# Five prefix products for fourteen, row statistics stored with the rows, shorter routing and new instruction orders in a four-layer sandwich kernel

## The chip, the cores and the metric

The program runs on one core of one Trainium2 chip. The core has five engines that run at the same time and wait for one another through semaphores: TensorE (PE in the profile, its weight loads PEld), VectorE (DVE), ScalarE (ACT), GpSimd (POOL) and SyncE (SP), which issues most of the DMAs. The metric is the device time of one execution in microseconds, as the median over runs.

## What is computed

The state is x, 8192 rows (tokens) of 256 values in fp32. Four sublayers follow one another; each normalizes x, computes, normalizes the result and adds it to x:

```python
x = x + ln(L0_attn(ln(x)))   # window attention, memory, gate, feed-forward
x = x + ln(L0_ffn(ln(x)))    # 8 experts, at most 512 rows each, GELU
x = x + ln(L1_attn(ln(x)))   # linear attention: relu(q), relu(k), kv = k^T v per batch
x = x + ln(L1_ffn(ln(x)))    # 8 experts, at most 1024 rows each, ReLU
```

Both expert layers route a row to the expert with the largest logit. Its place in the expert's buffer is the number of earlier rows with the same expert, a running count over all rows:

```python
onehot = one_hot(argmax(logits), 8)
rank = sum((cumsum(onehot, axis=0) - onehot) * onehot, axis=-1)
keep = rank < capacity
```

## The kernel before

Rows are handled in 16 groups of 512, a group as four tiles of 128 rows, side by side in one SBUF tile. Matrix products take fp32 operands as a high and a low part (`fh` and `fl`, for instance): ACT copies the high part, DVE subtracts it from the value to get the low part, and PE adds three products (`three`). Every engine has its own program, written out by hand in the order in which its instructions run; nothing reorders them, so a wait of one instruction holds all that stand behind it on that engine. The results of PE go through a ring of three PSUM units (`unit` takes the next one and waits until the third last is free again) and one fixed unit, `acc`.

The stages, one after the other:

- **Memory stage** (to about 270 us): two products and a Gram matrix over all groups.
- **Group loop** (about 270 to 1030 us): steps `s` over 16 groups, in which five groups are worked on at once. Group `s` is in the feed-forward (`ff_in`, `w2`, and DVE's `low`, `added`), group `s+1` at the gate (`gates`, `merged`, `weighed`, `combined`, `stats_2nd`, `affine_2nd`), group `s+2` in the window attention (`scores`, `masked`, `exponent`, `attend`, `attended`, `stats_1st`, `affine_1st`), groups behind `s` at the last norms (`affine_3rd`, `stats_4th`, `new_x`, `stats_5th`) and at the routing: `t_t`, `logits`, `route1` (argmax, one-hot `oht`), `prefix` (counts), `route2` (slots), `scatter` (four indirect DMAs into `d_p`). `doubled` writes the normalized row `df`, which SP stores in `d_x1` (`d_x` in the profile).
- **First expert stage** (about 1040 to 1240 us): eight blocks of 512 rows. `expert_out`, `expert_stats`, `expert_norm` and `expert_sum` make the new rows `eq`, and POOL's `expert_put` scatters them into `d_x1`.
- **Pair loop** (about 1250 to 1625 us): the linear attention, two groups a step. `load_x1` reads rows of `d_x1` as `xA`; `stats_l` and `nmean_l` (DVE) and `root` (POOL) make their mean and scale; `xl_norm` (ACT), `xl_t`, `queries`, `keys`, `state` (the sum kv in `acc`) follow. A pair is a batch: when its kv is complete, `kw_high` (ACT) and `kw_low` (DVE, the tile `small`) split it, and `att_out` of that pair needs it. Then come `stats_o`, `o_norm`, `new_x` and the second routing.
- **Second expert stage** (about 1630 to 2028 us): 16 blocks of 512 rows.

`prefix` makes the counts of a group's four tiles and of the whole group, 5 x 8 columns, each block as its own sum of products of `ones` or `tri` (a triangle of ones) with 8 columns of `oht`, 14 products in all:

```python
for i in range(5):
    ops = [(ones, k) for k in range(min(i, 4))] + ([(tri, i)] if i < 4 else [])
```

At steps 1 and 2 of the pair loop the engines also prepare the weights of the next expert (`weights_high` on ACT, `weights_low` on DVE, L1529), in both kernels right behind the step's first query work.

## Time and profile before

| | |
|---|---|
| median of three runs | 2033.78 us (2031.81 to 2036.07) |
| profiled execution, its own time | 2030.01 us |
| its span | 2028.2 us |
| PE, DVE, ACT, POOL busy | 1811.3, 1519.0, 1045.4, 664.0 us |
| mean granted TensorE clock | 0.952 of full speed |

The page gives busy times over the span, the granted clock in 40 slices, and groups of instructions. Times of single rows are microseconds from the span's start. A matmul's duration in a row runs from its issue to its end, and successive matmuls overlap, so their spacing is read from the starts. A row in square brackets says how long the engine idled ahead of the instruction and which instruction ended that.

### The profile page before, as it was taken

To read this page: it belongs to the slowest core of one execution; us is meant where nothing else is said; L and a number is where in the kernel's file an instruction comes from. 1 tells how busy PE (TensorE), PEld (TensorE's weight loads), DVE (VectorE), ACT (ScalarE), POOL (GpSimd) and SP (SyncE) were. 2 spreads that over 40 slices of the span, in tenths; PEclk is the share of its full clock that TensorE was granted. 3 is DMA by queue.
4 is the path that set the end of the run, shared out by engine and by line. 5 is a ranking of instruction groups with operands and counts; after the bars stand their busy time and mean duration, and the time that the engine had idled before them with its cause. 6 is when DMAs were issued, how large, how long until landed. Compare 5 with 4: busy or idle time off the path is not lost.

```text
span 2028.2 us, 31566 instructions
## 1 busy us (share of the span) xinstructions
PE 1811.3 (89%) x11506; PEld 1602.6 (79%) x11506; DVE 1519.0 (75%) x4023; ACT 1045.4 (52%) x1711; POOL 664.0 (33%) x872
## 2 busy tenths in 40 slices
PE   5888978999999999999759995879999589999996
PEld 4677867888888888888649994768888579999995
DVE  5666636999899999999838874679999656666663
ACT  4554633555555555555636652545555245555552
POOL 3343300132333343433433332024455513223232
PEclk9999998999999999999869997889999689999998
DMA  5545431011221211220224432123322222322210
GB/s 173 184 157 179 147 125 63 18 57 55 89 76 58 77 56 56 62 83 24 67 96 132 128 102 73 62 84 119 110 81 73 70 71 80 105 77 77 67 58 17
DMA packets 132610, 176.79 MB, mean 87 GB/s; under 512 B 11486, under 2 KB 115813, under 8 KB 132328
## 3 DMA queue, kind: packets, MB, share of 16 engines
q1 hardware_dynamic: 121704, 159.74, 25.0%
q0 software_dynamic: 10752, 15.04, 2.2%
q8 instruction: 92, 1.51, 0.3%
q14 instruction: 62, 0.51, 0.1%
HBM read 113.19 MB, written 76.41 MB: 93 GB/s over the span
## 4 chain that ended last, share of the span: by engine, by line
PE 71%; DVE 17%; issue 4%; DMA 4%; ACT 2%; POOL 2%; SPq 0%; POOLq 0%; DVEq 0%; ACTq 0%
PE ps L369 63%; PE ps L393 4%; DVE bst L1329 3%; DMA xa<-in_x 2%; PE ps L669 2%; POOL d_p L2123 1%; PE ps L658 1%; DVE fl L1538 1%; DVE dt L1593 1%; DVE xl L1598 1%; DVE dt L1588 1%; DVE xl L1609 1%; DVE smalls L1332 1%; DVE xl L1565 1%; DVE kl L1354 1%
## 5 line engine op out<-in xcount | busy, mean ns | idle before, releaser
L369 PE MATMUL ps<-wslotA,fh 128*128 128x256 f32 x1792 | 327.7, 284 | 0.0
L1538 DVE TENSOR_TENSOR fl<-fF,fh 128x512 fp32r<-128x512 f32 x320 | 215.1, 685 | 100.2 <-ACT fF L1022 98.9
L369 PEld LDWEIGHTS ps<-wslotA,fh 128*128 128x128 f32 x1792 | 284.1, 191 | 6.6
L2118 POOL TENSOR_TENSOR smalls<-smalls,powers 128x4 f32<-128x4 f32 x104 | 43.8, 421 | 678.2 <-DVE smalls L1332 678.1
L369 PE MATMUL ps<-wslotA,fl 128*128 128x256 f32 x896 | 253.5, 283 | 0.0
L369 PE MATMUL ps<-x2h,wslotA 128*128 128x512 f32 x512 | 180.7, 404 | 11.6 <-DVE xl L1565 11.6
L369 PEld LDWEIGHTS ps<-wslotA,fl 128*128 128x128 f32 x896 | 171.3, 191 | 0.0
L2123 POOL DMA_INDIRECT d_p<-pay,sut x128 | 147.6, 1153 | 62.1 <-issue 41.9
L1021 ACT ACTIVATE fh<-ps,b1e 128x512 fp32r<-128x512 f32 x128 | 88.3, 690 | 147.4 <-PE ps L369 118.8
L369 PE MATMUL ps<-wslotB,fh 128*128 128x256 f32 x768 | 139.9, 283 | 0.0
L369 PE MATMUL ps<-eh,wslotB 128*128 128x512 f32 x384 | 126.8, 396 | 4.1 <-DVE el L1725 4.1
L369 PE MATMUL ps<-eh,wslotA 128*128 128x512 f32 x384 | 126.6, 396 | 1.4 <-DVE el L1354 1.4
L1021 ACT ACTIVATE fh<-ps,cols 128x512 fp32r<-128x512 f32 x128 | 88.4, 691 | 71.1 <-PE ps L369 67.9
L369 PEld LDWEIGHTS ps<-wslotB,fh 128*128 128x128 f32 x768 | 121.8, 192 | 2.5
L369 PEld LDWEIGHTS ps<-x2h,wslotA 128*128 128x128 f32 x512 | 96.7, 189 | 32.0 <-DVE xl L1565 12.6
L2119 POOL TENSOR_TENSOR smalls<-smalls,powers 128x4 f32<-128x4 f32 x104 | 117.1, 1126 | 8.1
L369 PE MATMUL ps<-wslotB,fl 128*128 128x256 f32 x384 | 108.7, 283 | 0.0
L2123 POOL DMA_INDIRECT out_x<-eq,sut x64 | 73.3, 1145 | 95.1 <-DVE eq L1766 79.9
L369 PE MATMUL ps<-x2l,wslotA 128*128 128x512 f32 x256 | 100.6, 393 | 0.0
L1329 DVE BATCH_NORM_STATS2 bst<-xl 128x6 f32<-128x256 f32 x256 | 89.6, 413 | 0.4
L369 PEld LDWEIGHTS ps<-eh,wslotB 128*128 128x128 f32 x384 | 73.1, 190 | 19.3 <-DVE el L1725 4.5
L1022 ACT ACTIVATE fF<-ps,cols 128x512 f32<-128x512 f32 x128 | 87.9, 687 | 0.0
(340 smaller groups left out, 5068.3 us busy)
## 6 DMA issues: line engine op xcount, KB each, us to landing
stage<-in_w SPq DMA_DIRECT2D x16, 1024.0 KB
d_p<-pay SPq DMA_DIRECT2D x24, 528.0 KB, 5.2
pay<-d_p SPq DMA_DIRECT2D x24, 528.0 KB
xa<-in_x SPq DMA_DIRECT2D x16, 512.0 KB, 6.3
d_h<-hh SPq DMA_DIRECT2D x16, 512.0 KB, 4.6
d_h<-hl SPq DMA_DIRECT2D x16, 512.0 KB, 2.7
xl<-in_x SPq DMA_DIRECT2D x16, 512.0 KB, 4.1
hh<-d_h SPq DMA_DIRECT2D x16, 512.0 KB, 5.2
```

The lines of the kernel that those rows point to most:

```text
L369: return pe.matmul(o, a, b, start=start, stop=stop, skip_group_check=True)
L393: t = pe.transpose(ps[:, c * 512 + i * 128:c * 512 + i * 128 + 128], x[:, i * stride + c * 128:i * stride + (c + 1) * 128], ident)
L658: t = pe.transpose(ps[:, c * 512 + i * 128:c * 512 + i * 128 + 128], pv[:, i, c * 128:(c + 1) * 128], ident)
L669: t = pe.matmul(ps[:, i * 8:i * 8 + 8], x[:, c * 512 + i * 128:c * 512 + i * 128 + 128], w8[:, c, :], start=c == 0, stop=c == 1)
L1021: act.activation(fh[n % 2][:, half(k)], u.ap[:, half(k)], func, bias=b)
L1022: t = act.activation(fF[n % 2][:, half(k)], u.ap[:, half(k)], func, bias=b)
L1329: marks.append(mark(ve.bn_stats(b[:, i, :], x[:, i, :])))
L1332: t = ve.bn_aggr(mv[:, i, :], b[:, i, :])
L1538: ve.tensor_tensor(fl[n % 2][:, half(k)], fF[n % 2][:, half(k)], f32(fh[n % 2][:, half(k)]), ALU.subtract).then_inc(S["low"], 1)
L2118: last(po.tensor_tensor(t[:, 8:12], mv_of(t)[:, :, 1], eps, ALU.add))
L2119: po.tensor_tensor(t[:, 12:16], t[:, 8:12], mhalf, ALU.pow).then_inc(signal, 1)
L2123: po.indirect_dma_start(dst, bass.IndirectOffsetOnAxis(idx[:, i:i + 1], 0), src[:, i, :], None, bounds_check=bound, oob_is_err=False).then ...
```

## The change

**Prefix.** The one product of `tri` with all 32 columns, and four products of `ones` with the columns moved by one to four tiles to the right, give the same 40 columns.

**Routing.** `route1` makes the coded argmax in one instruction instead of two. `route2` compares the count, which now starts at the expert's offset (`base`), with the end of the expert's buffer (`ends`), two instructions instead of three.

**Statistics in the row.** A row of `d_x1` has 258 values: the row, its mean and its variance. In the group loop POOL's `root5` works them out from what it has (four instructions more, less one wait moved) and ACT copies them in behind `df`. In the first expert stage DVE takes the statistics of the new rows in `expert_sum`. In the pair loop `stats_l` and `nmean_l` are gone from DVE; POOL's `root_l` takes mean and variance from the loaded row. The tiles `df`, `eq` and `xA` grow to 4 x 258 values and others move to make room.

**Attention by halves.** `attend(g)` becomes `attend(g, 0)` and `attend(g, 1)`, each a unit of the ring finished before the next is taken; DVE's `attended` is split likewise, with `combined` between the halves.

**Orders.** All five programs of the group loop and of the pair loop are written in a new order, and both loops run one step less on PE and DVE, since the routing of a group starts a step earlier.

```diff
             def prefix(which, g):
                 pe.wait_ge(S["oh"], 16 * which + g + 1)
                 ps = unit("PF", which, g)
                 oh = oht[:, g % 2, :]
-                for i in range(5):
-                    ops = [(ones, k) for k in range(min(i, 4))] + ([(tri, i)] if i < 4 else [])
-                    for n, (m, k) in enumerate(ops):
-                        t = pe.matmul(ps[:, i * 8:i * 8 + 8], m, oh[:, k * 8:k * 8 + 8], start=n == 0,
-                                      stop=n == len(ops) - 1)
+                mm(ps[:, 0:32], tri, oh, True, False)
+                for d in range(1, 5):
+                    t = mm(ps[:, 8 * d:40], ones, oh[:, 0:40 - 8 * d], False, d == 4)
                 t.then_inc(S["pf"], 1)
...
-            def attend(g):
-                pe.wait_ge(S["ex"], g + 1)
-                pe.wait_ge(S["halo"], g // 2 + 1)
+            def attend(g, k):
+                if k == 0:
+                    pe.wait_ge(S["ex"], g + 1)
+                    pe.wait_ge(S["halo"], g // 2 + 1)
                 x, p = xl[g % 4], sc[g % 2]
-                units = [unit("AV", g, k) for k in range(2)]
+                ps = unit("AV", g, k)
...
             def expert_sum(n):
...
-                ve.tensor_tensor(q, q, pay_v[p % 3][:, :, 0:256], ALU.add).then_inc(S["eres"], 1)
+                t = ve.tensor_tensor(q, q, pay_v[p % 3][:, :, 0:256], ALU.add)
+                if n < E:
+                    stats(q, rows258(eq[n % 2])[:, :, 256:258], S["eres"], [mark(t)] * 4)
...
-            def stats_l(g):
-                stats(xv(xA[g % 2]), mv_of(sm(8, g)), S["var_l"], [(ld_x1[g % 2], 16 * (g // 2 + 1))] * 4)
...
+            def root_l(g):
+                t, b, x = sm(8, g), sm(9, g), rows258(xA[g % 2])
+                po.wait_ge(ld_x1[g % 2], 16 * (g // 2 + 1))
+                last(po.tensor_tensor(t[:, 8:12], x[:, :, 257], epsc, ALU.add))
+                po.tensor_tensor(b[:, 4:8], x[:, :, 256], mone, ALU.mult)
+                last(po.tensor_tensor(t[:, 12:16], t[:, 8:12], mhalf, ALU.pow))
+                po.tensor_tensor(b[:, 0:4], b[:, 4:8], t[:, 12:16], ALU.mult).then_inc(S["nm_l"], 1)
...
-            for s in range(-3, len(GROUPS) + 3):
+            for s in range(-3, len(GROUPS) + 2):
                 if s in GROUPS:
                     ff_in(s, 0, 0)
                     ff_in(s, 0, 1)
                     ff_in(s, 1, 0)
                     ff_in(s, 1, 1)
...
+                if s - 2 in GROUPS:
+                    logits(0, s - 2, tT, gwT)
+                if s + 2 in GROUPS:
+                    attend(s + 2, 0)
+                    attend(s + 2, 1)
                 if s in GROUPS:
                     ff_in(s, 2, 0)
                     w2(s, 0)
                     ff_in(s, 2, 1)
...
-                if s + 3 in GROUPS:
-                    load_xl(s + 3)
-                if s in GROUPS:
-                    load_xr(s)
+                if s >= 2 and s + 2 in GROUPS:
+                    load_xl(s + 2)
+                if s - 1 in GROUPS and s >= 2:
+                    load_xr(s - 1)
```

The last lines are SP's in the group loop, the loop above them is PE's. In the pair loop the order of PE puts `state(2s+1, 1)`, the last part of a pair's kv, at the end of its own step. It stood behind `queries` of the next step, right ahead of the work that leads to `att_out`.

What stands on DVE ahead of the split of kv in the middle of the pair loop, before (`small` is the low part of kv, `xA` the loaded rows, `pay` the new rows, `lgx` and `cdt` the routing's small tiles):

```order
L1329 BN_STATS bst<-xA_128 128x6 x4
L1332 BN_AGGR smalls<-bst 128x2 x4
L1329 BN_STATS bst<-pay_56 128x6 x4
L1332 BN_AGGR pay_56<-bst 128x2 x4
L1668 TENSOR_TENSOR lgx<-ps,pay_55 128x32
L1673 TENSOR_REDUCE smalls<-lgx 128x4
L1674 TENSOR_TENSOR lgx<-lgx,smalls 128x32
L1676 TENSOR_SCALAR cdt<-lgx 128x32
L1677 TENSOR_TENSOR cdt<-cdt,desc 128x32
L1678 TENSOR_REDUCE smalls<-cdt 128x4
L1679 TENSOR_TENSOR oht<-cdt,smalls 128x32
L1354 TENSOR_TENSOR xAl_133<-ps,xAh_131 128x512 x2
L1809 TENSOR_TENSOR small<-ps,small 128x516
```

And in the changed kernel, at the same place:

```order
L1672 TENSOR_TENSOR lgx<-ps,pay_55 128x32
L1677 TENSOR_REDUCE smalls<-lgx 128x4
L1678 TENSOR_TENSOR lgx<-lgx,smalls 128x32
L1680 SCALAR_TENSOR_TENSOR cdt<-lgx,desc 128x32
L1682 TENSOR_REDUCE smalls<-cdt 128x4
L1683 TENSOR_TENSOR oht<-cdt,smalls 128x32
L1334 BN_STATS bst<-pay_56 128x6 x4
L1337 BN_AGGR pay_56<-bst 128x2 x4
L1806 TENSOR_TENSOR small<-ps,small 128x516
L1359 TENSOR_TENSOR xAl_132<-ps,xAh_130 128x512 x2
L1780 TENSOR_SCALAR qF<-ps 128x1024
```

The statistics of `xA` are gone, the routing is one instruction shorter, and the split of kv stands ahead of the low part of the next group's rows and of the next queries.

POOL in the middle of the group loop, before (L2118 and L2119 are the two instructions of a `root`, L2123 a `scatter`, the rest are ends of `root5`):

```order
L2163 TENSOR_TENSOR s5t<-s5t,powers 128x4
L2118 TENSOR_TENSOR smalls<-smalls,powers 128x4
L2119 TENSOR_TENSOR smalls<-smalls,powers 128x4
L2123 DMA d_p<-pay_55,sut 4096x264 x4
L2118 TENSOR_TENSOR smalls<-smalls,powers 128x4
L2119 TENSOR_TENSOR smalls<-smalls,powers 128x4
```

And in the changed kernel, where the scatter stands behind the roots of the third, fourth and second norm, right ahead of that of the first norm:

```order
L2103 TENSOR_TENSOR smalls<-smalls,powers 128x4
L2104 TENSOR_TENSOR smalls<-smalls,powers 128x4
L2108 DMA d_p<-pay_55,sut 4096x264 x4
L2103 TENSOR_TENSOR smalls<-smalls,powers 128x4
L2104 TENSOR_TENSOR smalls<-smalls,powers 128x4
L2132 TENSOR_TENSOR s5t<-pay_54,powers 128x4
```

The scatter moved from behind one root to behind three, so the root of the first norm, which `affine_1st` waits for, now follows four DMA issues.

## Rows read from the trace of the kernel before

**Rows 1.** The page: span, busy time by engine, granted clock by slice.

```profile
span 2028.2 us, 31566 instructions
PE 1811.3 (89%) x11506; PEld 1602.6 (79%) x11506; DVE 1519.0 (75%) x4023; ACT 1045.4 (52%) x1711; POOL 664.0 (33%) x872
...
PEclk9999998999999999999869997889999689999998
```

**Rows 2.** Windows: stretch and length, busy by engine (instructions), clock, DMA share, GB/s.

```profile
543.60:894.70 351.10, 342.52 (x2313) 302.14 (x2312) 321.58 (x901) 195.57 (x313) 130.81 (x192) 1.00 0.21 67
...
1395.60:1512.90 117.30, 109.83 (x780) 98.09 (x780) 110.58 (x364) 63.68 (x106) 56.99 (x67) 1.00 0.34 104
...
1311.00:1395.00 84.00, 71.45 (x459) 63.61 (x457) 68.58 (x212) 42.56 (x68) 24.68 (x32) 0.91 0.29 89
...
1100.00:1200.00 100.00, 100.00 (x647) 91.11 (x646) 83.38 (x173) 64.87 (x105) 33.19 (x26) 1.00 0.41 126
```

**Rows 3.** Timeline of DVE, the group loop's last addition at two successive steps.

```profile
543.65 1.22 DVE L1614 TENSOR_TENSOR xl<-xl,ps 128x1024 f32<-128x1024 f32 x1
...
587.54 1.22 DVE L1614 TENSOR_TENSOR xl<-xl,ps 128x1024 f32<-128x1024 f32 x1
```

**Rows 4.** Waits in 543.6:894.7: who waited, total us, times, longest.

```profile
PE ps L369 <- DVE xl L1565: 8.6, 8, 1.3
...
DVE gt L1581 <- PE ps L369: 16.7, 16, 1.3
```

**Rows 5.** Waits of PE in 1240:1620, the pair loop.

```profile
PE ps L369 <- DVE small L1809: 28.2, 7, 11.1
...
PE ps L369 <- DVE qF L1783: 3.3, 4, 0.8
```

**Rows 6.** Timeline of PE: first of a prefix's 14 products, and what follows.

```profile
1445.55 0.17 PE L680 MATMUL ps<-oht,tri 128*128 128x8 bf16 x1
...
1445.90 0.37 PE L369 MATMUL ps<-kvh 128*128 128x258 f32 x1
```

**Rows 7.** Timeline of DVE in the pair loop.

```profile
1434.49 0.69 DVE L1809 TENSOR_TENSOR small<-ps,small 128x516 fp32r<-128x516 f32 x1
...
1445.47 1.40 DVE L1329 BATCH_NORM_STATS2 bst<-xA 128x6 f32<-128x256 f32 x4
...
1447.06 1.20 DVE L1783 TENSOR_SCALAR qF<-ps 128x1024 f32<-128x1024 f32 x1
...
1474.08 0.69 DVE L1809 TENSOR_TENSOR small<-ps,small 128x516 fp32r<-128x516 f32 x1
```

**Rows 8.** Timeline of DVE, two successive small instructions of the routing.

```profile
715.26 0.18 DVE L1676 TENSOR_SCALAR cdt<-lgx 128x32 f32<-128x32 f32 x1
715.48 0.19 DVE L1677 TENSOR_TENSOR cdt<-cdt,desc 128x32 f32<-128x32 f32 x1
```

**Rows 9.** Timelines of DVE and PE at pair step 1.

```profile
1302.77 2.36 DVE L1529 TENSOR_TENSOR wslotA<-stage,wslotA 128x1024 fp32r<-128x1024 f32 x2 [6.08 <-ACT wslotA L889]
...
1308.55 0.80 PE L369 MATMUL ps<-small,qh 128*128 128x258 f32 x2 [8.10 <-DVE small L1809]
```

**Rows 10.** Timelines of POOL, DVE and ACT between first experts and pair loop.

```profile
1249.61 0.97 POOL L2123 DMA_INDIRECT d_x<-eq,sut  x1 [0.30 <-issue]
...
1256.35 1.40 DVE L1329 BATCH_NORM_STATS2 bst<-xA 128x6 f32<-128x256 f32 x4 [10.88 <-DMA xA<-d_x]
...
1259.67 2.07 ACT L893 ACTIVATE xnA<-xA,smalls 128x256 f32<-128x256 f32 x4 [19.57 <-DVE smalls L1775]
```

**Rows 11.** Timelines of PE and POOL at the group loop's end.

```profile
1013.00 3.58 PE L669 MATMUL ps<-gwT,tT 128*128 128x8 f32 x16 [13.28 <-ACT tT L889]
...
1022.73 3.58 PE L669 MATMUL ps<-gwT,tT 128*128 128x8 f32 x16 [1.88 <-ACT tT L889]
...
1035.90 0.97 POOL L2123 DMA_INDIRECT d_p<-pay,sut  x1 [0.30 <-issue]
```

**Rows 12.** DMA issues in 700:790: KB, median us to landing.

```profile
xl<-in_x SPq DMA_DIRECT2D x2, 512.0 KB, 4.0
```

**Rows 13.** Durations of a root's first instruction on POOL, ns min/median/max.

```profile
L2118 POOL TENSOR_TENSOR smalls<-smalls,powers x104: 190/223/1219, 294.6 to 1597.0; 128x4 f32<-128x4 f32 x104
```

More of the change, by code:

```diff
@@ L811, in tensor_program @@
                     memory(2)
+                if s - 1 in GROUPS:
+                    t_t(0, s - 1)
+                if s in GROUPS:
+                    w2(s, 2)
+                if s + 1 in GROUPS:
+                    x2_t(s + 1)
+                if s - 2 in GROUPS:
+                    prefix(0, s - 2)
+                if s in GROUPS:
+                    w2(s, 3)
+                if s + 3 in GROUPS:
+                    scores(s + 3)
+                if s == -3:
+                    memory(3)
+                if s + 2 in GROUPS:
+                    x1_t(s + 2)
             for n in range(-1, E):
@@ L829, in tensor_program @@
             values_folded()
-            for s in range(-1, len(PAIRS) + 3):
+            for s in range(-1, len(PAIRS) + 2):
                 if s in PAIRS:
                     queries(2 * s)
-                if s - 3 in PAIRS:
-                    prefix(1, 2 * s - 5)
                 if s - 2 in PAIRS:
-                    t_t(1, 2 * s - 4)
-                if s - 1 in PAIRS:
-                    state(2 * s - 1, 1)
-                if s - 2 in PAIRS:
-                    logits(1, 2 * s - 4, tTO, wgT)
+                    prefix(1, 2 * s - 4)
                 if s in PAIRS:
-                    xl_t(2 * s + 1)
                     keys(2 * s, 1)
@@ L846, in tensor_program @@
                     att_out(2 * s - 2, 1)
-                if s + 1 in PAIRS:
-                    xl_t(2 * s + 2)
                 if s in PAIRS:
-                    keys(2 * s + 1, 0)
-                    queries(2 * s + 1)
+                    state(2 * s, 0)
                 if s - 2 in PAIRS:
                     t_t(1, 2 * s - 3)
-                    prefix(1, 2 * s - 4)
-                if s in PAIRS:
-                    state(2 * s, 0)
                 if s - 1 in PAIRS:
@@ L860, in tensor_program @@
                 if s in PAIRS:
+                    keys(2 * s + 1, 0)
+                if s + 1 in PAIRS:
+                    xl_t(2 * s + 2)
+                if s - 2 in PAIRS:
+                    logits(1, 2 * s - 3, tTO, wgT)
+                if s in PAIRS:
                     keys(2 * s + 1, 1)
                     state(2 * s, 1)
+                    queries(2 * s + 1)
+                if s - 1 in PAIRS:
+                    t_t(1, 2 * s - 2)
                 if s + 1 in PAIRS:
@@ L865, in tensor_program @@
                 if s - 2 in PAIRS:
-                    logits(1, 2 * s - 3, tTO, wgT)
+                    prefix(1, 2 * s - 3)
                 if s in PAIRS:
                     state(2 * s + 1, 0)
+                if s - 1 in PAIRS:
+                    logits(1, 2 * s - 2, tTO, wgT)
+                if s in PAIRS:
+                    state(2 * s + 1, 1)
+                if s + 1 in PAIRS:
+                    xl_t(2 * s + 3)
             for n in range(E - 1, 3 * E):
@@ L1248, in scalar_program @@
             values_folded()
-            for s in range(-2, len(PAIRS) + 2):
+            for s in range(-1, len(PAIRS) + 2):
                 if s in PAIRS:
@@ L1866, in vector_program @@
             memory(2)
-            for s in range(-3, len(GROUPS) + 3):
+            for s in range(-3, len(GROUPS) + 2):
                 if s in GROUPS:
@@ L1920, in vector_program @@
                 if s + 1 in GROUPS:
+                    combined(s + 1)
+                if s + 2 in GROUPS:
+                    attended(s + 2, 1)
+                if s + 1 in GROUPS:
+                    stats_2nd(s + 1)
+                if s in GROUPS:
+                    low(s, 2, 0)
+                if s + 2 in GROUPS:
+                    stats_1st(s + 2)
+                if s in GROUPS:
+                    low(s, 2, 1)
+                if s + 1 in GROUPS:
                     affine_2nd(s + 1)
@@ L1981, in vector_program @@
             values_folded()
-            for s in range(-2, len(PAIRS) + 3):
+            for s in range(-1, len(PAIRS) + 2):
                 if s in PAIRS:
@@ L2316, in store_df @@
                 sp.wait_ge(S["df"], g + 1)
-                load(tok_rows(d_x1, g), xv(df), S["st_df"])
+                load(tok_rows(d_x1, g), rows258(df), S["st_df"])
             def load_pay(n):
@@ L2342, in load_x1 @@
                     sp.wait_ge(S["xn_l"], g - 1)
-                load(xv(xA[g % 2]), tok_rows(d_x1, g), ld_x1[g % 2])
+                load(rows258(xA[g % 2]), tok_rows(d_x1, g), ld_x1[g % 2])
             def load_xb(g):
@@ L2347, in load_xb @@
                     sp.wait_ge(S["tn"], G + g - 1)
[L2348 removed]
+                load(xv(xb[g % 2]), tok_rows(d_x1, g)[:, :, 0:256], ld_xb[g % 2])
             def store_out(g):
```

396 lines of the change are left out of this document (176 added, 220 removed).

## Prediction

> **What bounds the kernel now.** I read the page first [rows 1]: PE is busy for 1811 of 2028 us and DVE for 1519, and the granted clock falls below its full 2.4 GHz level only in a few slices. So the time is PE's, and what the change can win is PE's work, PE's waits and the slow clock behind long waits. Which of them there is differs by stage, so the windows come next [rows 2].
>
> In the group loop eight steps take 351.1 us, 43.9 each, as the starts of the same addition in two successive steps show [rows 3]. PE is busy for 342.5 of them (42.8 a step) and DVE for 321.6 (40.2 a step). The list of waits for that window has one wait of PE, 1.07 us in each step, for L1565, which is `attended` [rows 4]: `attend` takes two ring units together, and the next `ff_in` needs one of them back. DVE waits 2.1 us a step for the gate products. So the group loop is bound by PE, with DVE close behind.
>
> In the first expert stage PE has no gap at all (100 of 100 us) and DVE is busy for 83%.
>
> In the pair loop a pair takes 39.6 us [rows 7], 39.1 on average over three; PE is busy for 36.6 of that and DVE for 36.9, and what DVE does not work is mostly the gap between dependent small instructions. Here DVE sets the pace. PE's waits say the same: 28.2 us for `small`, the split of kv on DVE, and 3.3 us for `qF` [rows 5]. Two of the seven waits for `small` are long, 8.1 us at step 1 and 11.1 us the longest; at step 1 DVE itself waited 6.1 us for ACT's part of an expert's weights, with `kw_low` queued behind it [rows 9].
>
> **Prefix and routing.** Fourteen products start within 0.35 us, 25 ns apart [rows 6]. Five, the first with 32 columns, should take 0.13 to 0.2 us. I take 0.2 us saved a group, 3.2 us in each loop, where PE is the bound; the ends are 0 and 0.28 a group. The routing loses two small instructions a group at 0.22 us from start to start [rows 8]: 0.44 us a group on DVE.
>
> **Statistics.** `stats_l` holds DVE for 1.59 us a group (from its start to the start of `qF` [rows 7]) and `nmean_l` for about 0.2, so a pair loses 3.6 us on DVE. In the first expert stage each of eight blocks gets 1.59 us more on DVE. Its cover is PE's 100%: DVE has 3.9 us left of the 23 us that a block takes at 83%, so I cost it at nothing; without that cover it would be 13 us. POOL gets three more small instructions in `root5`; it is busy for 131 of 351 us, so this is hidden as well.
>
> Between the two stages the chain is exposed: the last `expert_sum`, four scatters, the load, statistics, scale, ACT's norm. The statistics now stand ahead of the scatters (+1.6 us). Behind the load, 3.3 us pass from the first statistic to ACT's norm [rows 10]; `root_l` replaces that by four dependent POOL instructions, between 0.9 us (at 0.22 each) and those 3.3 us. I take 1.8, and the sum of this place is zero.
>
> The row of `d_x1` grows from 1024 to 1032 bytes and no longer starts at a multiple of 256 bytes. By the last scatter's end (1250.6) and DVE's resumption, the wait for the load is 5.8 us [rows 10]. The Trainium skill (DMA: Bandwidth & Descriptors, How a descriptor splits into AXI transactions) says that a transfer that starts off a 256-byte boundary also fetches the bytes back to that boundary. An estimate by that page is some 36 beats a row instead of 32, so 0.8 us more on those 5.8 us, where I add nothing. No run here shows it yet.
>
> **Attention by halves and the group loop's order.** With halves, the first unit comes free while the second is in use, and in the new order `ff_in(s, 2, 0)` takes the unit that `logits` had, not one of the attention. The 1.07 us should go. New bound of a step: 43.9 - 1.1 - 0.2 = 42.6 us on PE, against 40.2 - 0.4 = 39.8 us on DVE, which leaves 2.8 us for DVE's own waits where it has 3.7 now. Twelve steps run at full width, so 12 x 1.07 = 12.9 us; I leave 2 us for new waits and take 10.9. The ends are 0 and 13. What is queued behind the moved pieces: on DVE `combined` and `stats_2nd` behind `attended`, on POOL the root of the first norm behind four scatter issues, on SP the row load and `load_xr` behind `load_h`, now followed by `store_df`. Laid out by hand with the rows' durations, every one arrives before PE needs it, by one to some ten us.
>
> **The end of the group loop.** Two rounds of logits stand one after the other here, 9.7 us apart, the first behind a wait of 13.3 us, and then the last scatter at 1035.9 [rows 11]. In the new order the first of these rounds is over a step earlier, so the last group's routing starts right behind its `new_x`. One round less is 9.7 us; POOL, which must still issue the last three scatters and a longer `root5`, takes some of it back. I take 6, the ends are 3 and 10. The pair loop's end has the same chain, but there the transpose of the last group still stands behind the prefix of the one before it: 0.
>
> **The pair loop.** DVE has 36.9 - 3.6 - 0.9 = 32.4 us of work a pair, PE 36.6 - 0.4 = 36.2. PE becomes the bound with 3.8 us of cover. The kv path is shorter too: `state(2s+1, 1)` comes before the transpose, `queries` and `keys` of the next step, all of which cover the split, and `kw_low` stands ahead of `weights_low` instead of behind it. Of the 31.5 us of waits [rows 5] I leave 10: 2.5 at each of steps 1 and 2, where DVE still does 2.4 us of weights and waits for ACT ahead of them, and 5 at the loop's two ends. That gives 21.5. Behind the long waits the clock is low: 0.91 over 84 us [rows 2], 7.6 us' worth, of which I take 3 back. With the prefix the loop wins 27.7 us. The ends are 10 (only the relief of DVE, the rest turned into other waits) and 38 (all waits, all of the clock).
>
> **Sum.** 10.9 + 3.2 + 6 + 27.7 = 47.8 us. The profiled execution took 2030.0 us, so 1982.2; the median of the runs stands 3.8 us above it, so I predict 1986 us for the median.
>
> **Rivals.**
> 1. *DVE or POOL becomes the bound of the group loop.* For it: DVE is within 2.8 us of PE, and the root of the first norm now follows four DMA issues with `affine_1st`, `x1_t` and the gate behind it. Against it: DVE waits 2.1 us a step for PE today and loses work. If DVE's waits exceed 2.8 us a step the gain of 14.1 goes: 2000 us. A root's first instruction takes 0.19 to 1.22 us [rows 13], so one that falls badly is 1.0 us late, which over twelve steps is 12 us, and 1998 us. The Trainium skill (GPSIMD Engine Reference, Key points) says that GpSimd shares its SBUF interfaces with VectorE and is held up by VectorE instructions with two SBUF inputs; such instructions fill DVE in this loop, and by that rule the late case would be the usual one. The spread in the row agrees with it, the median of 0.22 us does not make it usual.
> 2. *The pair loop's waits move instead of going.* Four units of `att_out` now stand nearly together, with only `state` and a transpose between them, and each is held until DVE has read it; queued behind them on DVE are the key and query parts that `state` waits for. For it: today's longest waits were of this kind. Against it: 3.8 us of cover. Gain of 10 instead of 27.7: 2004 us.
> 3. *Slower than before: the rows of x arrive late.* `load_xl` can only start when `new_x` has freed the tile, and lands 4.0 us later [rows 12]; then come ACT's norms and the transpose, which in the new order stand a fair way earlier behind `new_x` (my layout leaves 2 us). Every microsecond above that is lost in each of some 14 steps. To turn 48 us of gain into a loss of more than 4 it takes 3.7 us a step, a landing after about 9.7 us instead of 4.0. 2040 us.
> 4. *Both 1 and 2*: 2018 us. That the change does nothing is excluded for the work it removes, but both removals could fall under other waits, which is this case.
>
> **Chances.** Forecast 0.63, with a range of its own of 1970 to 1998; rival 1 0.14, rival 2 0.11, rivals 1 and 2 together 0.06, rival 3 0.06. The lower end takes the best of each part: 13 + 4.5 + 10 + 38 = 65 us, hence 1968, and I go to 1966. The upper end takes in rivals 1 and 2 and stops short of both together: 2012. A measurement of this kernel tells a change from none at about 0.2%, 4 us. Faster by more than that 0.91, within it 0.02, slower 0.07.
>
> **What would show it.** In the changed kernel's profile: a period of 42.5 to 42.8 us in the group loop with no wait for L1565's successor; a period near 36.5 us a pair with waits for `small` under 8 us in all; PE still without gaps in the first expert stage; the second stage's loads about 6 us sooner behind the last addition of the group loop; five prefix products within 0.2 us. The forecast is wrong if PE shows a new wait of over 1 us in every step of either loop, for `affine_1st`, the rows of x, `qF` or `kvl`.

## The result and the profile after

The changed kernel takes 1984.7 us (median of 4 runs, 1981.3 to 1987.3) where the kernel before takes 2033.7 us (median of 4, 2031.8 to 2036.1): a ratio of 0.9762, with a 95% interval of 0.9747 to 0.9777. The forecast was 1986 us. The profiled execution of the changed kernel has a span of 1985.5 us against the 2028.2 us of [rows 1].

The page of the changed kernel, the same lines as before: span, busy time of PE and DVE, and the granted clock in 40 slices.

```profile
span 1985.5 us, 30949 instructions
PE 1805.3 (91%) x11218; PEld 1593.6 (80%) x11218; DVE 1495.1 (75%) x3879; ACT 1072.4 (54%) x1749; POOL 664.8 (33%) x953
...
PEclk8989998999999999999959999899999699999998
```

PE is busy for 6 us less and the span is 42.7 us shorter, so most of the gain is idle time of PE. Windows of the changed kernel: the group loop, four pairs of the pair loop, the first experts.

```profile
543.60:894.70 351.10, 351.10 (x2326) 309.90 (x2325) 327.01 (x915) 220.23 (x343) 134.56 (x233) 1.00 0.20 66
...
1365.56:1508.73 143.17, 143.17 (x970) 128.59 (x969) 132.07 (x399) 83.91 (x141) 65.52 (x101) 1.00 0.35 104
...
1100.00:1200.00 100.00, 100.00 (x651) 91.41 (x650) 90.08 (x200) 64.77 (x105) 48.52 (x26) 1.00 0.40 129
```

PE has no gap in any of them. In [rows 2] it had 8.6 us in the first window, and 7.5 us in 117.3 us of pairs. DVE is at 93% of the group loop and 92% of the pairs. The list of waits of the changed kernel for PE, over the pair loop and its end, has little left of the 28.2 us for `small` [rows 5]:

```profile
PE ps L371 <- DVE base L1694: 5.5, 1, 5.5
PE ps L661 <- DVE pay L1655: 3.9, 1, 3.9
PE ps L371 <- DVE oht L1683: 3.3, 3, 1.5
PE ps L672 <- ACT tTO L890: 3.1, 3, 1.2
PE ps L371 <- DVE small L1806: 1.9, 1, 1.9
```

**Where the time went, by stages.** The same events are found in both traces: the first product of the score matrix on PE, the first of the group loop's additions on DVE, the first transpose of expert tokens in each expert stage, and the first transpose of the pair loop. The timelines of DVE and PE of the changed kernel have them here; the first row is the score product, then the first and the fourteenth of the sixteen additions, the first experts, the pair loop, the second experts.

```profile
291.52 1.99 PE L371 MATMUL ps<-qb,qa 128*128 128x256 f32 x8 [0.84 <-DVE qb L1500]
...
380.63 1.22 DVE L1618 TENSOR_TENSOR xl<-xl,ps 128x1024 f32<-128x1024 f32 x1 [1.21 <-PE ps L371]
...
933.91 1.21 DVE L1618 TENSOR_TENSOR xl<-xl,ps 128x1024 f32<-128x1024 f32 x1
...
1033.29 1.97 PE L395 MATMUL ps<-ident,etk 128*128 128x128 f32 x8 [15.82 <-DVE etk L1714]
...
1253.22 1.94 PE L395 MATMUL ps<-ident,xnA 128*128 128x128 f32 x8 [23.47 <-issue]
...
1587.99 1.97 PE L395 MATMUL ps<-ident,etk 128*128 128x128 f32 x8 [13.70 <-DVE etk L1714]
```

The differences of these starts, and of the same ones in each other trace of this study, make one table (us; "setup" is up to the score product, "fill" from there to the first addition, "groups" from there to the first experts' transpose, "rest" the second experts to the end of the span):

| kernel | setup | fill | groups | experts 1 | pairs | rest | time of the runs, ratio |
|---|---|---|---|---|---|---|---|
| before | 282.7 | 89.8 | 670.8 | 218.4 | 368.8 | 397.6 | 2033.7 |
| changed | 291.5 | 89.1 | 652.7 | 219.9 | 334.8 | 397.5 | 1984.7, 0.9762 |
| e1 | 288.5 | 89.0 | 670.0 | 218.8 | 367.2 | 398.3 | 2032.4, 0.9973 |
| e2 | 288.9 | 90.1 | 655.6 | 219.8 | 339.4 | 399.1 | 1992.8, 0.9777 |
| e3 | 287.2 | 88.7 | 652.7 | 218.2 | 349.6 | 398.2 | 1998.9, 0.9813 |
| e4 | 282.1 | 89.6 | 673.4 | 218.6 | 368.6 | 397.7 | 2035.6, 0.9989 |
| e5 | 284.7 | 90.1 | 652.7 | 221.0 | 353.7 | 398.0 | 2003.6, 0.9866 |
| e6 | 291.3 | 94.6 | 657.6 | 218.4 | 336.7 | 397.8 | 1996.5, 0.9825 |
| e7 | 284.3 | 90.1 | 652.7 | 236.0 | 335.9 | 397.7 | 1999.5, 0.9851 |
| e9 | 285.5 | 89.7 | 652.7 | 219.5 | 336.9 | 398.5 | 1985.7, 0.9777 |
| e10 | 289.9 | 88.5 | 710.7 | 217.9 | 337.0 | 397.9 | 2040.8, 1.0043 |
| e11 | 290.5 | 89.1 | 652.2 | 219.5 | 333.7 | 398.5 | 1985.2, 0.9766 |
| e12 | 284.8 | 89.9 | 652.7 | 219.5 | 332.1 | 397.5 | 1983.3, 0.9778 |
| e13 | 288.8 | 88.6 | 652.1 | 218.4 | 331.7 | 398.8 | 1980.8, 0.9751 |

The groups gained 18.1 us and the pairs 34.0 us. Experts 1 took 1.5 us more. The setup is 8.8 us longer in this execution, of which 2.1 belong to the change and the rest to the clock (last section). A stage that was left alone repeats closely in the traces: the groups take 652.7 us in each of the six with the changed kernel's loop (670.8 and 670.0 in before and e1); fill, experts 1 and rest repeat within 2 us, and within 2.2 us for the pairs: 334.8 to 337.0 in the five traces with the changed kernel's pair loop (changed, e6, e7, e9, e10), 336.3 on average. That mean is what the experiments on the pair loop are held against; by it the pairs gained 32.5 us. So effects of 2 us and more are read from this table, though each row is one execution, and the ratios, with intervals some 3 to 4 us to each side, confirm the larger ones. Each ratio is against executions of the kernel before that were taken beside it, whose medians lie between 2031.0 and 2037.0 us, so kernels are compared by ratio and not by their medians. For the small effects the two sources can part: by the ratios e1 and e4 gain 5.5 and 2.2 us, by the table without the setup e1 gains 2.1 and e4 loses 2.5.

### The profile page after: what moved, and what is told of

It is laid out like the page before. It is cut to its first block, busy times and chain, and to the rows that moved or that the text cites. A ratio compares the mean times of both kernels' runs of the same rounds, so it can differ in the third digit from the quotient of the medians.

```text
span 1985.5 us, 30949 instructions
## 1 busy us (share of the span) xinstructions
PE 1805.3 (91%) x11218; PEld 1593.6 (80%) x11218; DVE 1495.1 (75%) x3879; ACT 1072.4 (54%) x1749; POOL 664.8 (33%) x953
## 4 chain that ended last, share of the span: by engine, by line
PE 80%; DVE 9%; DMA 4%; issue 3%; ACT 2%; POOL 2%; SPq 1%; POOLq 0%; DVEq 0%; ACTq 0%
PE ps L371 72%; PE ps L395 4%; PE ps L672 2%; DMA xa<-in_x 2%; DVE bst L1334 1%; PE ps L661 1%; POOL d_p L2108 1%; DVE f1l L1406 1%; SPq L2249 1%; DVE kl L1359 1%; DMA stage<-in_w 0%; DVE row_l L1413 0%; DVE hl L1422 0%; DMA stage<-in_W2T 0%; DMA pay<-d_p 0%
## 5 line engine op out<-in xcount | busy, mean ns | idle before, releaser
L2103 POOL TENSOR_TENSOR smalls<-smalls,powers 128x4 f32<-128x4 f32 x88 | 27.5, 312 | 584.3 <-DVE smalls L1337 584.2
L2108 POOL DMA_INDIRECT d_p<-pay,sut x128 | 153.1, 1196 | 103.3 <-issue 51.7
L371 PE MATMUL ps<-x2h,wslotA 128*128 128x512 f32 x512 | 172.1, 397 | 0.2 <-DVE x2l L1359 0.2
L371 PE MATMUL ps<-eh,wslotB 128*128 128x512 f32 x384 | 127.4, 398 | 4.1 <-DVE el L1727 4.1
L1022 ACT ACTIVATE fh<-ps,cols 128x512 fp32r<-128x512 f32 x128 | 88.7, 693 | 49.1 <-PE ps L371 45.3
L2104 POOL TENSOR_TENSOR smalls<-smalls,powers 128x4 f32<-128x4 f32 x88 | 96.4, 1096 | 6.9
L1348 DVE SCALAR_TENSOR_TENSOR xl<-xl,smalls,rows 128x256 f32<-128x256 f32 x192 | 80.0, 479 | 14.2 <-POOL smalls L2104 14.2
```

Source lines behind the costliest of these rows:

```text
L371: return pe.matmul(o, a, b, start=start, stop=stop, skip_group_check=True)
L1022: act.activation(fh[n % 2][:, half(k)], u.ap[:, half(k)], func, bias=b)
L1348: marks = [mark(ve.scalar_tensor_tensor(x[:, i, :], x[:, i, :], m[:, i:i + 1], gain, ALU.subtract, ALU.mult)) for i in range(4)]
L2103: last(po.tensor_tensor(t[:, 8:12], mv_of(t)[:, :, 1], eps, ALU.add))
L2104: po.tensor_tensor(t[:, 12:16], t[:, 8:12], mhalf, ALU.pow).then_inc(signal, 1)
L2108: po.indirect_dma_start(dst, bass.IndirectOffsetOnAxis(idx[:, i:i + 1], 0), src[:, i, :], None, bounds_check=bound, oob_is_err=False).then ...
```

## The experiments

**e1 and e2: the prefix alone, and the prefix undone.** e1 is the kernel before with this edit, e2 the changed kernel with it reversed.

```diff
-                for i in range(5):
-                    ops = [(ones, k) for k in range(min(i, 4))] + ([(tri, i)] if i < 4 else [])
-                    for n, (m, k) in enumerate(ops):
-                        t = pe.matmul(ps[:, i * 8:i * 8 + 8], m, oh[:, k * 8:k * 8 + 8], start=n == 0,
-                                      stop=n == len(ops) - 1)
+                mm(ps[:, 0:32], tri, oh, True, False)
+                for d in range(1, 5):
+                    t = mm(ps[:, 8 * d:40], ones, oh[:, 0:40 - 8 * d], False, d == 4)
```

> The kernel before with the five-product prefix and nothing else. Theory: a prefix loses 0.20 us of PE (14 products in 0.35 us become 5 in 0.15 us). In the group loop PE is the bound with one wait a step, so 3.2 us go there; in the pair loop PE waits for DVE anyway, so 0 to 3.2 us. 3.2 to 6.4 us less in all, a ratio of 0.997 to 0.9985, the group loop's period 43.7 instead of 43.88 us. Rival: PE's time is refilled by the ring wait of L1565, nothing is gained, period 43.88, ratio 1.000.

> The changed kernel with the old fourteen-product prefix. Theory: PE has no idle time in either loop of the changed kernel, so all 0.20 us a group come back: 6.4 us more, 1991 us, ratio 0.979, period of the group loop 42.87 instead of 42.67 us, of a pair 36.2 instead of 35.8. Rival: the small products start under other work, and nothing changes: 1985 us, ratio 0.976.

In the changed kernel the five products take 0.15 us from the first one's start to the next work, as its timeline of PE shows, against 0.35 us in [rows 6]:

```profile
1565.67 0.21 PE L371 MATMUL ps<-oht,tri 128*128 128x32 bf16 x1 [1.52 <-DVE oht L1683]
1565.72 0.25 PE L371 MATMUL ps<-oht,ones 128*128 128x32 bf16 x4
1565.82 1.95 PE L661 MATMUL ps<-ident,pay 128*128 128x128 f32 x8
```

In e1 the rival held in the group loop: the period stays at 43.88 us, and the wait for the sum with the attention (L1563 in e1) takes what PE saved. PE's waits in eight steps of e1, where [rows 4] has 8.6 us:

```profile
PE ps L369 <- DVE xl L1563: 10.4, 8, 1.5
```

The stages give 2.1 us in all without the setup, 1.6 of it among the pairs; the ratio, 0.9973 (0.9961 to 0.9985), is 5.5 us with a lower end of 3. Where the rest of it would be was not found. In e2, where PE has no idle time, the same 0.20 us shows: the period (over the nine steady steps) goes from 42.55 to 42.77 us, the groups take 2.9 us more and the pairs 3.1. The ratio, 0.9777, can't tell e2 from e9 (0.9777) or the changed kernel. So in the group loop 0.2 us a step is worth nothing beside a wait of PE's in each step and its full size once the wait is gone.

**e3: the old order in the pair loop.** The loop over `PAIRS` of PE, ACT, DVE and POOL and the one of SP are those of before; DVE's has no `stats_l` and `nmean_l`, and POOL's calls `root_l`.

```diff
-                    root(sm(8, 2 * s + 4), (S["var_l"], 2 * s + 4 + 1), S["rs_l"])
+                    root_l(2 * s + 4)
...
-                    stats_l(2 * s + 4)
...
-                    nmean_l(2 * s + 4)
```

(against the kernel before; everything outside these loops is the changed kernel's.)

> The changed kernel with all five engines' old order in the pair loop; the statistics still come with the rows, and the group loop keeps its new order. Theory (the orders' share): the pair loop gained 34 us between the two traces; 10 of them are DVE's relief, 24 the order, which puts the small dependent product's operands ahead of PE's need. So 24 us more, 2009 us, ratio 0.988, with waits for small of over 12 us in all. Rival (the relief's share): the 3.6 us a pair that DVE lost are what mattered, and with them any order runs at PE's pace: 1985 to 1992 us, ratio under 0.980.

The pairs take 349.6 us, 13.3 more than with the new order and 19.2 less than before; the ratio of 0.9813 (0.9798 to 0.9828) is 10 us above the changed kernel's. Both are between the two expectations. Where the time lies says more. The window of four steady pairs of e3, and PE's waits for `small` in e3 from the loop's start (1246.84) up to there:

```profile
1374.30:1517.20 142.90, 142.84 (x970) 128.83 (x969) 131.30 (x398) 84.41 (x140) 82.51 (x99) 1.00 0.33 104
```

```profile
PE ps L371 <- DVE small L1802: 15.9, 2, 9.3
```

The old order runs the steady pairs at PE's pace, 35.7 us each and without a wait, as soon as DVE is relieved. The new order gains nothing there (35.8 us). It gains at the start, and as the edit moves all five engines at once, which of the moved pieces did it is not shown. From the loop's first transpose to the third start of `kw_low` it needs 112.3 us (113.1 in e9), e3 127.4. (`kw_low` stands elsewhere in a step, which moves some 3 us between this stretch and the loop's end.)

**e5: the statistics on DVE again, in the new order.**

```diff
+                if s + 1 in PAIRS:
+                    stats_l(2 * s + 3)
...
+                    nmean_l(2 * s + 3)
+                    stats_l(2 * s + 4)
...
+                    nmean_l(2 * s + 4)
```

(in DVE's loop, and POOL's `root_l` is `root` of the variance again.)

> The changed kernel, its orders kept, with the row statistics and the mean times root computed on DVE in the pair loop again (they also still come with the rows, and the copy is not used). Theory (DVE's relief is worth what it relieves beyond PE's pace): DVE's work in a pair goes from 33.0 to 36.6 us, PE's stays 35.8, so DVE sets the pace again: 0.8 us a pair is the floor, 7 us, and with a few waits behind late small instructions 7 to 15 us, so the stage from the first transpose to the second experts takes 342 to 350 us instead of 335. Rival (the order alone does it): under 3 us. Rival (the relief does it all): 19 us or more, as in the kernel with the old order, where the relief alone had taken 369 to 350 us.

The pairs take 353.7 us, 17.4 more than with the copy, more than the 7 to 15 us that I gave. The intervals between starts of `kw_low` are 37.4, 44.8, 39.2, 38.3, 37.9, 36.5 and 34.4 us. The steady ones, where I had the floor of 0.8, are 0.7 to 3.4 us above 35.8. The first `kw_low` stands 39.3 us behind the loop's start instead of 32.8, and PE waits 5.4 us for `xAl` there (1.4 in the changed kernel), since the statistics now stand in front of the first norms. The two large parts of the change now stand without each other and together (us for the pairs): neither 368.8, relief without the order 349.6, order without the relief 353.7, both 336.3. 19.2 and 15.1 add up to 34.3, and both together gave 32.5. Both e3 and e5 keep the shorter prefix and the shorter routing, so what these two give is in both numbers; the prefix's share (1.6 us in e1, 3.1 in e2) is about what the sum is too large by. The routing's share was not measured alone. Neither part makes the other worthless, as each rival theory had it.

**e4 and e9: halves alone, and halves undone.** e4 is the kernel before with `attend` and `attended` by halves, called one behind the other. e9 is the changed kernel with PE taking both units first:

```diff
-                ps = unit("AV", g, k)
+                if k == 0:
+                    units[:] = [unit("AV", g, n) for n in range(2)]
+                ps = units[k]
```

> The kernel before with the attention by halves on PE and DVE, in the old order (the two halves stand one behind the other). Theory: the wait for L1565 is one of order, since ff_in still takes the first unit of attention directly behind the prefix, and halves alone change nothing: period 43.88 us, wait 1.07 us a step, ratio 1.000. Rival: the first half comes free while the second is in use, the wait goes, 12 us less, ratio 0.994.

> The changed kernel, its orders kept, with PE taking both of the attention's ring units before the first product, as the kernel before did. Theory: since halves alone gave nothing in the old order, the new order removed the wait, and halves matter to neither: period 42.56 us, no wait of PE in the loop, ratio as the changed kernel's. Rival: halves and order are both needed; a wait of about 1 us a step comes back, 12 us more.

In e4 the period is 43.9 to 44.1 us and a wait of up to 1.0 us is still there in each step; in e9 it is 42.55 us and PE waits for nothing in eight steps. So the order removed the wait and the halves on PE had no part in it; alone they made a step 0.11 us longer. DVE still reads the two halves apart in e9, with `combined` between them, so that piece counts as part of the order. PE's waits in eight steps of e4:

```profile
PE ps L369 <- DVE xl L1566: 6.9, 8, 1.0
```

**e6: more work for DVE in the group loop.** The result is the same, the statistics are computed three times.

```diff
             def stats_1st(g):
                 u = [ring.of("AV", g, k) for k in range(2)]
+                for n in range(2):
+                    stats(xw(xl[g % 4]), mv_of(sm(0, g)), S["again"], ...)
```

> The changed kernel with the first norm's statistics computed three times instead of once in the group loop: 2 x 1.59 us more on DVE in each step, in the chain from the attention to the first norm. Theory: DVE's work is 39.8 us a step, PE's 42.6; the extra makes it 43.0, so DVE becomes the bound by 0.4 us a step, and since its waits can't vanish altogether the period rises to 43.0 to 44.5 us, 5 to 25 us more in all. Rival: the chain is slack, DVE catches up in its waits, period 43.0, 5 us. Rival of my forecast (cover was an illusion because DVE's place in the chain is exposed): the whole 3.2 us a step appears, period 45.8, 38 us more.

The period is 42.9 us, at the floor of 39.8 + 3.2, where the first rival had put it. A window of e6 within the group loop shows both engines full at once:

```profile
550.00:890.00 340.00, 338.84 (x2213) 296.40 (x2212) 335.38 (x1006) 212.75 (x333) 115.14 (x214) 1.00 0.20 68
```

The groups take 4.9 us more. Another 5.5 us is in the fill, where nothing covers the chain from the attention to the first norm. Together that is 10.4 us, and the runs have 10.8 between e6 and e9, within my 5 to 25.

**e7: more work for DVE in the first experts.**

```diff
                 if n < E:
+                    if n < E - 1:
+                        for _ in range(2):
+                            stats(q, rows258(eq[n % 2])[:, :, 256:258], S["again"], ...)
                     stats(q, rows258(eq[n % 2])[:, :, 256:258], S["eres"], ...)
```

> The changed kernel with the statistics of the expert rows computed three times in seven of the eight blocks of the first expert stage: 2 x 1.59 us more on DVE in each. Theory (the cover that the prediction named): DVE has 2.3 us of 23.4 left in a block with the one computation, the two more take 3.2, so DVE becomes the bound by 0.9 us a block, 6 us more in all, and the stage from the first transposed tokens to the first transpose of the pair loop takes 226 instead of 220 us. Rival (no cover, the statistics stand in the chain of each block): 3.2 us a block, 22 us. Rival (the waits in which DVE idles can't be used): 10 us or more.

The stage takes 236.0 us, 16 more than in the changed kernel, where my theory said 6 and the last rival 10 or more: 2.3 us in each of seven blocks, where the first of three statistics costs none (PE has no gap in 1100:1200 above). The window of e7 shows that DVE does not fill up as it did in e6, and PE's waits in its blocks name the lower half that DVE delivers:

```profile
1100.00:1200.00 100.00, 94.29 (x604) 84.12 (x605) 93.90 (x240) 58.28 (x93) 42.96 (x24) 1.00 0.39 121
```

```profile
PE ps L371 <- DVE fl L1543: 12.8, 13, 2.0
```

**e10: the rows of x late.**

```diff
                 if g >= 4:
                     sp.wait_ge(S["tn"], g - 3)
+                    sp.wait_ge(S["var1"], g)
```

> The changed kernel with the load of x for a group waiting for the first norm's statistics too, which DVE finishes 5.9 us after the sum that frees the tile. The norm that uses the rows starts 0.6 us after they land now, and the transpose behind it is due some 6 us after that norm. Theory, as I put it: some 2 us of slack, everything above is lost in each step, so 3.9 us a step over 13 steps, 51 us more, and the kernel is as slow as before. Rival: ACT's queue order (the late norm holds back the two hidden pieces behind it) makes all of 5.3 us appear, 69 us. Rival: the slack on PE takes most of it: under 15 us.

The runs give 2040.8 us, a ratio of 1.0043 (1.0026 to 1.0060): slower than before. The period is 47.54 us on average, 5.0 above 42.55, and the groups take 58 us more, between my 51 and the 69 of the first rival. In eight steps of e10 ACT waits 43.6 us for the rows, 5.45 a step, and 5.0 of them arrive at the period:

```profile
PE ps L395 <- ACT xl L894: 26.2, 8, 3.9
...
ACT xl L894 <- DMA xl<-in_x: 43.6, 8, 6.1
```

**e11, e12 and e13: towards a better version.** The timelines of the changed kernel show two things still in the way. At pair step 1 DVE waits for an expert's weights, with the reading of a prefix's counts right behind it, and PE's wait carries the name of `base`. (`kw_low`, which the expectation of e12 names too, ran 8 us ahead of it, at 1322.17, and next at 1365.56.) The rows of DVE, PE and SP:

```profile
1330.52 2.36 DVE L1534 TENSOR_TENSOR wslotA<-stage,wslotA 128x1024 fp32r<-128x1024 f32 x2 [4.73 <-ACT wslotA L890]
...
1334.46 0.77 PE L371 MATMUL ps<-small,qh 128*128 128x258 f32 x2 [5.54 <-DVE base L1694]
...
1319.80 1.59 SPq L2249 DMA_DIRECT2D stage<-in_w  x1
```

That load stands behind a store and loads of rows on SP's queue, while its tile is free at 1294.7. e12 moves it ahead (SP's loop):

```diff
             for s in range(-1, G // 2 + 2):
+                if s in (0, 1):
+                    weights(19 + s)
                 for i in range(2):
...
-                if s in (0, 1):
-                    weights(19 + s)
```

e11 reorders the last steps: the routing of group 14 before the third norm of group 15, `scatter(0, 13)` and `scatter(0, 14)` before `root5(0, 15)`, `weights_low(3)` behind the last `route2`, and `t_t(1, 15)` before `prefix(1, 14)`. Its main lines, on POOL:

```diff
                     root(sm(2, s - 1), (S["var3"], s - 1 + 1), S["rs3"])
+                    if s == 16:
+                        scatter(0, 13)
                     root(sm(3, s - 1), (S["var4"], s - 1 + 1), S["rs4"])
```

> The changed kernel with other orders in the last steps of the two loops: the routing of group 14 before the third norm of group 15, its scatters before the root of group 15, a weights' split behind the last routing, and in the pair loop the last transpose before the prefix of group 14. Theory (the ends are chains of POOL issues, DVE's small instructions and PE rounds): 2.6 us less behind the group loop, 1.5 us less behind the pair loop, 4 us in all, ratio 0.974. Rival (the scatters' landing or the last route sets the end anyway): under 1 us.

> The changed kernel with the load of an expert's weights in pair steps 0 and 1 ahead of that step's loads and stores of rows on the DMA queue of SP, where it stood behind them. Theory: the only long wait of PE within the pair loop, 5.5 us put down to base, is really this load, issued at 1319.8 although its tile is free at 1294.7; DVE waits 4.7 us for it with the prefix's reader and kw_low behind it. It goes: 5.5 us less, 1979 us, ratio 0.9735, the second interval between the starts of kw_low 36 to 38 us instead of 43.4. Rival (something else in that step is late anyway): under 2 us, the interval over 41 us.

> Both edits of the two kernels before this one together. Theory: the places are apart, so the gains add: 9.5 us, 1975 us, ratio 0.971 to 0.972. Rival: they do not add, since the earlier weights only move the wait to the pair loop's end: 0.974 or more.

e12: the load is issued at 1288.8, the interval falls from 43.4 to 40.5 us, and the pairs take 332.1 us instead of 336.3 (2.7 less than in the changed kernel's own trace). The runs don't show it: the ratio is 0.9778 (0.9759 to 0.9796), where 0.9735 was expected and the changed kernel has 0.9762. Half of the wait is left, and now it is ACT's own copy that DVE waits for (the list of PE's waits and DVE's timeline of e12):

```profile
PE ps L371 <- DVE base L1694: 2.9, 1, 2.9
```

```profile
1321.83 2.36 DVE L1534 TENSOR_TENSOR wslotA<-stage,wslotA 128x1024 fp32r<-128x1024 f32 x2 [2.07 <-ACT wslotA L890]
```

e11: 0.5 us less in the groups and 2.6 among the pairs. Behind the group loop the last scatter's issue ends 31.1 us after the last addition instead of 32.3, but the tokens come 38.4 us after it instead of 38.9: less than half of what the queue of scatters gave was passed on. Its ratio, 0.9766 (0.9749 to 0.9783), shows no gain over the changed kernel either. e13 ran fastest: 1980.8 us, a ratio of 0.9751 (0.9733 to 0.9768), against 1984.7 and 0.9762 (0.9747 to 0.9777) for the changed kernel. It beats the kernel before. Against the changed kernel the stages without the setup show 4.4 us (1689.6 against 1694.0), of which 2.0 lie in fill and experts 1, which the edits don't touch, and the intervals overlap, so that gain is not settled. Both edits together were expected to give 9.5.

## Why the prediction was right, and where it was not

The span fell by 42.7 us in the profiled execution, by 51.4 without the setup, and the medians by 49.0. The sum said 47.8. The profiled execution lost some 6.6 us in the setup to the clock; with them it is 49.3. That the total is so near is partly luck: the pair loop gave 6.3 us more than its term, and against it stand 1.4 us less in the group loop's steps, 0.6 less at its end, 1.5 more in the first experts and 2.1 more in a stretch that the sum left out, while the fill took 0.7 less. The terms in turn.

- **Group loop, right.** Period forecast 42.5 to 42.8 us, measured 42.55 in nine steady steps (the one before them takes 43.7). DVE is busy for 39.7 us a step, where 39.8 was forecast. PE waits for nothing. 10.9 + 3.2 us was forecast for the steps; from the first addition to the fourteenth the changed kernel needs 553.3 us, before 566.0, which is 12.7. The mechanism as I put it joined two causes, halves and order. e4 and e9 show that PE's halves had no part in it and the order was needed; that it is `ff_in` taking another unit of the ring fits this, but was not tried by itself.
- **End of the group loop, right.** 6 us forecast. From the fourteenth addition to the experts it was 104.8 us (938.6 to 1043.4) and is 99.4: 5.4. PE's 13.3 us and the second round of [rows 11] have become one wait of 12.7 us and one round.
- **Prefix, right in size.** 0.20 us a group. It is not a term of its own, though: e1 shows that without the new order it vanishes in the group loop.
- **Statistics in the first experts, right in cost, with the wrong idea of the cover.** Costed at nothing, and PE has no gap. I gave DVE 3.9 us to spare in a block, 2.3 behind the first extra. e7 took 3.2 more and lost 2.3 a block instead of 0.9. The free time in this stage can't be used to the end, while in the group loop it could (e6).
- **Transition, right.** The sum was zero; experts 1 with the transition take 217.9 to 219.9 us in the traces that left it alone, 219.0 on average, against 218.4 to 218.8 in before, e1 and e4. `root_l` takes 1.8 us from the rows' landing to ACT's norm, the value I had chosen. The wait for the load, from the last scatter's end to the engine that resumes, was 5.8 us [rows 10] and is 6.3 in this execution (1242.95 to 1249.28). The Trainium skill (DMA: Bandwidth & Descriptors, How a descriptor splits into AXI transactions) gives a cost to rows that start off a 256-byte boundary, which an estimate by that page put at 0.8 us here. The traces together do not bear it out. With rows of 1024 bytes the wait is 5.77, 5.89 and 5.82 us (before, e1 and e4); with rows of 1032 it is 5.47 to 6.33 in the eleven other traces, 5.79 on average. So the longer rows cost nothing here that can be told from the spread, and the 0.6 us of the one execution is part of it.
- **Pair loop, right mechanism, size off.** 27.7 us forecast, 34.0 measured (32.5 by the mean of five traces). The windows of the stage, before and changed:

```profile
1261.85:1630.61 368.76, 307.96 (x2080) 275.32 (x2081) 298.87 (x960) 173.84 (x281) 147.37 (x174) 0.90 0.28 87
```

```profile
1253.22:1587.99 334.77, 299.87 (x1936) 268.64 (x1936) 271.51 (x801) 172.27 (x281) 130.89 (x201) 0.92 0.32 96
```

PE idles for 34.9 us instead of 60.8, 25.9 less, where I had 21.5. It is busy for 8.1 us less, where I had 3.2 for the prefix and 3 for the clock; how the 8.1 divide was not measured. "Only the relief of DVE" was my low end, 10 us, and e3 measured 19.2. It is enough for PE's full pace in the steady pairs with the old order. I had left 10 us of waits; of the 31.5 us there are 1.9 left under the old name and 5.5 under `base`, 7.4 in all. Of the 19.2, 6.4 lie ahead of the third `kw_low` and 12.8 behind it. The new order's part is 13 to 15 us, nearly all of it in the first three steps, where e3 still waits 15.9 us for `small`. The steady steps, where I saw the order at work, got nothing from it. The pace is 35.8 us a pair, 0.7 below my 36.5. PE's 36.6 us of busy time a pair [rows 2] was not pure work, because e3 does the same products, less 0.4 us of prefix, in 35.7. My high end of 38 us was also added up wrongly: 31.5 of waits, 7.6 of clock and 3.2 of prefix are 42.3.
- **Prologue, a term that the sum left out.** From the row on `cols`, a few products ahead of the score product, the changed kernel needs 11.4 us up to the score product, in each of its traces, and the kernel before 9.3: PE waits 2.0 us for `g` there. These 2.1 us of loss are the change's. The other 6.6 us of the setup are not (last section).
- **Rival 1 (DVE becomes the bound of the group loop)** did not come. e6 puts a price on it: the 2.8 us of cover are real, and 3.2 us more raise the period by 0.38. A root's first instruction still takes between 0.19 and 1.09 us over the whole trace, 0.20 in the median, but none of the 33 in the window of the group loop takes over 0.56 (in the kernel before the longest there was 1.16), and PE has no wait there. So the rule of the Trainium skill (GPSIMD Engine Reference, Key points), by which the late case would be the usual one, did not decide here.
- **Rival 2 (the waits move)** did not come; the only trace of it is the 5.5 us put down to `base`, which is a load that stood behind others.
- **Rival 3 (the rows of x late)** did not come: the rows land before ACT asks for them. e10 shows that it would have been about what I priced: 5.9 us later makes 2040.8 us. My slack of 2 us was too large. The load starts 5.9 us later, ACT waits 5.45 of them and the period takes 5.0, so the slack was 0.9.

## What to carry to other kernels

A small saving on the engine that bounds a loop can be worth nothing while that engine also waits for a ring unit in every iteration; remove the wait first, and the saving counts in full, as it did here. Split a gain into the steady iterations and the filling of the loop before giving it to a cause: here relief of the second engine paid mostly in the steady pairs, the order only while the loop filled. A wait that is put down to a small result may be a large transfer queued ahead of it on the waited-for engine; look one instruction further back there, then at the queue that issued the transfer.

## What was not expected of the hardware

The setup's clock varies from execution to execution. Windows of the same 60 us of the kernel before, of e1 and of the changed kernel (the first column after the instruction counts is PE's mean granted clock):

```profile
90.00:150.00 60.00, 51.02 (x266) 42.12 (x265) 38.84 (x100) 34.02 (x72) 21.10 (x23) 1.00 0.53 178
```

```profile
90.00:150.00 60.00, 51.00 (x237) 41.48 (x238) 36.17 (x89) 29.05 (x63) 20.44 (x20) 0.91 0.48 160
```

```profile
90.00:150.00 60.00, 50.82 (x231) 40.96 (x230) 36.55 (x87) 28.57 (x62) 18.29 (x19) 0.89 0.47 157
```

PE is busy for 51 us in each, but at the lower clock it gets less done. A clock of 0.89 over 60 us is 6.6 us' worth. The row of PE on `cols`, up to which the two codes take the same time, starts at 273.45 us in before, at 279.22 in e1, which shares its code here, and at 280.08 in the changed kernel; it is at 272.81 in e4 and 273.38 in e12, which has the changed kernel's code. In e4 and e12 the clock of this window is 1.00 too. The mean over the whole setup hides this (0.96 in e1, e4 and e12), because it also counts stretches in which PE stands still. PE is busy for 84% of the setup and often waits, and part of it runs at the slow level of 1.2 GHz, not in the same slices from trace to trace. What tips the clock in one execution and not in another was not found. In the group loop, where PE hardly waits, the clock is 1.00 in each of the windows shown. These 6.6 us are more than most terms of this study, so a table of stages with the setup apart resolves what the medians of the runs can't.

DVE and PE can both be full at once: 98.6% and 99.7% in e6's group loop, which I had not thought possible with dependent work between them.
